# Attention: reciprocal spread and values in one bank, both issued behind a tile's second head, divisions sooner

## The chip, the cores and the metric

The kernel runs on one core of one Trainium2 chip. The metric is the device time of one execution in microseconds (us); the kernel before takes 1476.72 us (median of three runs, 1476.59 to 1477.12).

## The reference

One pre-norm decoder layer on x of shape (4, 512, 512): self-attention with 16 heads of width 32, then a cross-attention whose weights come from a context of width 256, then a feed-forward block with 4-bit weights. The part that matters here is the self-attention:

```
q, k, v = layernorm(x) @ Wq, @ Wk, @ Wv         # 16 heads of width 32
scores  = einsum('bthd,bshd->bhts', q, k) * tril   # masked entries are 0, not -inf
attn    = softmax(scores / sqrt(512), axis=-1)
x       = x + einsum('bhts,bshd->bthd', attn, v) @ Wo
```

Masked scores are zero and not minus infinity, so each row's denominator also holds a term for the tokens beyond the diagonal, and the values of those tokens are added with that one weight.

## The kernel before, in words

**The four batches.** The kernel walks over four batches (`body(n, last)` on each engine). In each, a stretch of about 62 us holds the softmax and the products with the values; around it lie the projections for the next batch and the mixing of this one (`between`). After the last batch comes the feed-forward block, a long dense run of TensorE matmuls.

**Units.** The softmax stretch is cut into 16 units. Unit u stands for four heads (group u // 4) and one tile of 128 query tokens (i = u % 4). A tile sees (i + 1) * 128 keys, so the widths of its four heads j = 0..3 are 128, 256, 384 or 512. The order of work on each engine is written out by hand as steps (u, j); nothing reorders it.

**One head of one unit** goes through these instructions. `scores` (TensorE, L932) writes bank j. `row_max` (VectorE, L1603) takes the maximum, GpSimd negates it (`shift`, L766), ScalarE takes the exponential (`exp`, L1260) into `prob`. `turn` (TensorE, L943) transposes it in blocks of 128 into one of three rotating banks, and `turned` copies that to `prob_t`: ScalarE for heads 0 to 2 (L1276; heads 0 and 1 only where i is 3), VectorE for the others (L1613). `scores(u + 1, j)` waits for `exp(u, j)`, because both use bank j.

**Once for each unit:** `reciprocals` (VectorE, L1631) makes `r_col`, one reciprocal for each token and head. `recips` (TensorE, L973) spreads them over the 32 rows of each head, eight matmul records. ScalarE copies the result to `r_den` (`recip_out`, L1282). `values` (TensorE, L964) multiplies `prob_t` with V into bank 6, in the half u % 2, with a last part for the tokens beyond the diagonal (`v_zero`, made by GpSimd, L776), and VectorE's `divide` (L1641) multiplies that half with `r_den` into `o_sum`. `values(u)` waits for `divide(u - 1)`. After a group's last unit ScalarE (`out_head`, L1288) and GpSimd (`out_tail`, L782) split `o_sum` in two half-precision parts.

**Repacking.** Beside this, TensorE transposes packed feed-forward weights in two halves (`repack`, L1039), at i = 0; ScalarE copies the first half (L1296), VectorE the second (L1654).

**The rotating banks.** `turn_bank(slot)` is one of banks 4, 5 and 7, by slot modulo 3. Each `turn`, each repacked half and, in the kernel before, each spread reciprocal (`recip_slot`) takes the next slot, and waits until the slot three before has been read (`turn_read`). In a unit without repacking the order of slots is T0 T1 T2 T3 R, where T is a head's transposes and R the reciprocals of the unit before.

**The order on TensorE in unit u:** before each turn(u, j) comes scores(u + 1, j). Behind turn(u, 1) stand both halves of the repacking where i = 0; behind turn(u, 3) come recips(u - 1) and values(u - 1). On ScalarE, step (u, j) is exp(u, j), then a copy of an earlier head. recip_out(v) stands in step (v + 2, 1), out_head in step 0 of a unit with i = 2. On VectorE divide(v) stands in step (v + 3, 0). At the end of a batch, TensorE also transposes the next batch's normalised input (`spread`, L892), with a copy by ScalarE (L1237) and a difference by VectorE (L1588).

Of the kernel before, what the change touches and what calls it, by code (L numbers as in the profile page):

```python
# [46 lines left out]
P = 128  # L47
# [44 lines left out]
def decoder_layer(nc, x, ctx_1024, Wq, Wk, Wv, Wo, xWq, xbq, xWk, xbk, gate_p, gate_s, up_p, up_s, down_p, down_s, out):  # L92
    with ExitStack() as ctx:
# [162 lines left out]
        den_done, rcol_done, r_full, rden_out = (sem(n) for n in ("den_done", "rcol_done", "r_full", "rden_out"))  # L256
# [22 lines left out]
        def turn_slot(h):  # L279


            return h + 2 * (max(0, h - 2) // 16) + max(0, h // 4 - 1)
# [13 lines left out]
        def pack_slot(r, half):  # L296
            return (turn_slot(16 * r + 17) + 1 if r < HG - 1 else recip_slot(UNITS - 2) + 1) + half

        def recip_slot(u):
            return turn_slot(4 * u + 7) + 1 if u < UNITS - 1 else pack_slot(HG - 1, 1) + 1  # L300
# [4 lines left out]
        def turn_read(n, slot):  # L305

            for u in range(UNITS):
                if slot == recip_slot(u):
                    return rden_out, n * UNITS + u + 1
# [12 lines left out]
        AT_RECIP, AT_DIVIDE = 9, 12  # L322
        AT_SUMS, AT_TURNED, AT_RECIPROCALS = 1, 3, 2
        AT_OUT = 0
# [347 lines left out]
        def _(pool):  # L672
# [155 lines left out]
            def body(n, last):  # L828
                for u in range(UNITS):
                    r, i = u // TT, u % TT  # L830
                    for j in range(4):
                        shift(n, u, j)
                        if j == 1 and u > 0 and i > 0:
                            masked_values(n, u - 1)
                        if j > 0 and i > 1:
                            convert(n * (NB // B) + r, r, 3 * i + j - 7)
                        if j == 3 and i == 2 and r > 0:
                            out_tail(n, r - 1)
# [37 lines left out]
        def _(pe):  # L876
# [69 lines left out]
            def values(n, u):  # L946
# [4 lines left out]
                if u == 0:  # L951
                    pe.wait_ge(v_out, n * TT + TT)
                if u >= 1:
                    pe.wait_ge(o_done, n * UNITS + u)
# [12 lines left out]
            def recips(n, u):  # L967

                slot = recip_slot(u)
                pe.wait_ge(*turn_read(n, slot - 3))  # L970
                pe.wait_ge(rcol_done, n * UNITS + u + 1)
                for j in range(4):
                    mm = pe.matmul(turn_bank(slot)[32 * j:32 * j + 32, 0:P], r_col[:, u % 2, j:j + 1].to_broadcast([P, DH]), ident[:], start=True, stop=True)  # L973
                mm.then_inc(r_full, 1)
# [53 lines left out]
            def repack(n, r):  # L1028
                nb = n * (NB // B) + r
                pe.wait_ge(pk_conv, 6 * nb + 6)  # L1030
                for half in range(2):
                    pe.wait_ge(*turn_read(n, pack_slot(r, half) - 3))
                    bk = turn_bank(pack_slot(r, half))[:].bitcast(F16)

                    tiles = [[(0, 0), (1, 0)], [(0, 1), (1, 1)], [(2, 0), (3, 0)]] if half == 0 else \
                            [[(2, 1), (3, 1)], [(4, 0), (4, 1)], [(5, 0), (5, 1)]]
                    for q in range(3):
                        for e, (a, w) in enumerate(tiles[q]):
                            mm = pe.transpose(bk[:, 256 * q + P * e:256 * q + P * e + P], pk_16[:, a, P * w:P * w + P], ident16[:])  # L1039
                    mm.then_inc(pk_full, 1)  # L1040
# [163 lines left out]
            def body(n, last):  # L1204
                for u in range(UNITS):
                    for j in range(4):
                        if u + 1 < UNITS:
                            scores(n, u + 1, j)
                        turn(n, u, j)
# [3 lines left out]
                        if j == 1 and u == UNITS - 1:  # L1213
                            values(n, u - 1)
                        if j == 3 and u > 0:
                            recips(n, u - 1)
                            if u < UNITS - 1:
                                values(n, u - 1)
                        if j == 1 and u % TT == 0 and u > 0:
                            repack(n, u // TT - 1)  # L1220
                repack(n, HG - 1)
# [11 lines left out]
        def _(act):  # L1233
# [44 lines left out]
            def recip_out(n, u):  # L1278
                act.wait_ge(r_full, n * UNITS + u + 1)
# [763 lines left out]
```

## Time and profile before

| | |
|---|---|
| median of three runs | 1476.72 us |
| profiled execution, its own time | 1477.48 us |
| its span in the trace | 1475.80 us |
| TensorE clock granted | 0.999 of full speed |
| softmax stretches in the span | about 71 to 133, 203 to 265, 335 to 397, 467 to 527 us |
| TensorE busy, whole span | 1424.5 us (97%) |
| ScalarE, VectorE busy, whole span | 716.9 us (49%), 990.3 us (67%) |

The profile is one execution on the chip. Its page gives busy times for the whole span; the stretch that the change touches is a sixth of it, and the views below are of that stretch. A matmul's record is longer than the time until the next matmul starts, so a busy share of TensorE is not its load. The same holds in a smaller measure for ScalarE and VectorE: each record reaches some tenth of a microsecond into the next one. So the text works with the time from one start to the next.

### The profile page before, as it was taken

The numbers are of one execution on the slowest core, as the hardware profiler recorded it, in microseconds if no ns is written. First come the engines' busy times: TensorE is split into PE (matmuls) and PEld (weight loads), VectorE is DVE, ScalarE is ACT, GpSimd is POOL, SyncE is SP. The second block draws the span as 40 slices with busy tenths as digits, with TensorE's granted clock in tenths as the row PEclk, the third lists the DMA queues.
The fourth block names the chain that finished last, engine by engine and source line by source line (L and its number), as shares of the span: only waits on it lengthen the run. The fifth ranks groups of instructions, "written<-read, shape, count | busy, mean of one in ns | idle before, by whom it ended". The sixth has DMA issues, their size and how long they took to land.

```text
span 1475.8 us, 26841 instructions
## 1 busy us (share of the span) xinstructions
PE 1424.5 (97%) x8896; PEld 719.7 (49%) x8896; DVE 990.3 (67%) x2125; ACT 716.9 (49%) x1660; POOL 380.3 (26%) x691
## 2 busy tenths in 40 slices
PE   6999998998999999999999999999999999999999
PEld 3465456556645654344444444444444444444444
DVE  7786688668658767886566666665655756665533
ACT  5795279339716945344354353353343443533532
POOL 0053225204374436521221212112112211212100
PEclk9999999999999999999999999999999999999999
DMA  7564522352465521000100001001001001000011
GB/s 249 134 168 125 162 79 81 101 162 79 126 176 156 180 80 46 17 28 22 32 14 21 17 17 33 17 17 35 17 17 32 17 16 33 17 17 1 0 58 57
DMA packets 77309, 98.01 MB, mean 66 GB/s; under 512 B 8048, under 2 KB 60784, under 8 KB 76784
## 3 DMA queue, kind: packets, MB, share of 16 engines
q1 hardware_dynamic: 77168, 96.23, 21.3%
q8 instruction: 76, 1.25, 0.4%
q14 instruction: 65, 0.53, 0.1%
HBM read 68.94 MB, written 27.26 MB: 65 GB/s over the span
## 4 chain that ended last, share of the span: by engine, by line
PE 85%; ACT 5%; issue 5%; DVE 4%; POOL 1%; DMA 0%; ACTq 0%; POOLq 0%; DVEq 0%; SPq 0%
PE bank L879 25%; PE bank L881 24%; PE bank L880 24%; ACT prob L1260 3%; PE bank L943 3%; PE bank L964 2%; PE bank L932 1%; PE bank L892 1%; PE bank L1004 1%; PE bank L1019 1%; PE bank L973 1%; PE bank L1014 1%; ACT prob_t L1276 1%; DVE xt L1588 1%; PE bank L1025 1%
## 5 line engine op out<-in xcount | busy, mean ns | idle before, releaser
L879 PE MATMUL bank<-xs,G 128*128 128x512 f16 x896 | 339.8, 379 | 2.1 <-DVE c L1733 1.0
L880 PE MATMUL bank<-xs,G 128*128 128x512 f16 x896 | 339.6, 379 | 0.0
L881 PE MATMUL bank<-xs,G 128*128 128x512 f16 x896 | 339.6, 379 | 0.0
L1348 ACT COPY c<-bank 128x512 f32<-128x512 f32 x192 | 111.4, 580 | 219.9 <-PE bank L881 215.1
L1733 DVE TENSOR_TENSOR c<-bank,c 128x512 f32<-128x512 f32 x128 | 88.1, 689 | 193.4 <-PE bank L881 193.4
L879 PE MATMUL bank<-Wd,hid 128*128 128x512 f16 x512 | 194.1, 379 | 2.8 <-DVE X L1787 2.8
L881 PE MATMUL bank<-Wd,hid 128*128 128x512 f16 x512 | 194.0, 379 | 0.0
L880 PE MATMUL bank<-Wd,hid 128*128 128x512 f16 x512 | 194.0, 379 | 0.0
L751 POOL TENSOR_TENSOR c<-c,m 128x512 f32<-128x512 f32 x64 | 82.3, 1287 | 388.9 <-ACT c L1348 388.9
L1787 DVE SCALAR_TENSOR_TENSOR X<-bank,col,X 128x512 f32<-128x512 f32 x128 | 95.4, 749 | 101.5 <-PE bank L881 101.4
L1603 DVE CUSTOM_DVE_ANT_0 bank<-bank,mask,col 128x128 f32<-128x128 f32 (+3 forms) x256 | 139.1, 548 | 23.4 <-issue 17.3
L1260 ACT ACTIVATE prob<-bank,nmx 128x128 f32<-128x128 f32 (+3 forms) x256 | 146.9, 582 | 0.7
L879 PEld LDWEIGHTS bank<-xs,G 128*128 128x128 f16 x896 | 87.7, 98 | 113.5 <-ACT c L1348 6.1
L881 PEld LDWEIGHTS bank<-xs,G 128*128 128x128 f16 x896 | 87.7, 98 | 105.7
L880 PEld LDWEIGHTS bank<-xs,G 128*128 128x128 f16 x896 | 87.7, 98 | 103.1
L943 PE MATMUL bank<-ident,prob 128*128 128x128 f32 x640 | 111.9, 277 | 12.9 <-ACT prob L1260 3.8
L1371 ACT CAST hid<-c 128x512 f16<-128x512 f32 x128 | 79.2, 619 | 90.3 <-DVE c L1747 87.2
L1363 ACT ACTIVATE c<-c,col 128x512 f32<-128x512 f32 x96 | 69.4, 723 | 94.1 <-DVE c L1733 94.1
L766 POOL TENSOR_TENSOR nmx<-zero,mx 128x1 f32<-128x1 f32 x256 | 51.1, 200 | 234.7 <-DVE mx L1603 208.6
L1753 DVE TENSOR_TENSOR hid<-c,hid 128x512 f16<-128x512 f32 x128 | 86.1, 712 | 25.7 <-ACT hid L1371 25.7
L708 POOL TENSOR_TENSOR w_sum<-w_full 128x384 f32<-128x384 f32 (+1 forms) x30 | 22.1, 738 | 314.0 <-DVE w_full L1714 313.8
L943 PEld LDWEIGHTS bank<-ident,prob 128*128 128x128 f32 x640 | 76.0, 140 | 30.8 <-issue 19.3
(192 smaller groups left out, 2408.3 us busy)
## 6 DMA issues: line engine op xcount, KB each, us to landing
stack<-qk_dram SPq DMA_DIRECT2D x128, 128.0 KB, 3.4
sc_in<-scale_t SPq DMA_DIRECT2D x30, 384.0 KB
qk_dram<-qk SPq DMA_DIRECT2D x32, 256.0 KB, 2.7
packed_t<-pk_t SPq DMA_DIRECT2D x32, 192.0 KB, 2.0
pk_in<-packed_t SPq DMA_DIRECT2D x30, 192.0 KB
X<-in_x_dram SPq DMA_DIRECT2D x4, 1024.0 KB, 5.9
pk_in<-L_ffn_gate_W_packed_dram SPq DMA_DIRECT2D x16, 256.0 KB, 2.7
pk_in<-n_L_ffn_up_W_packed_dram SPq DMA_DIRECT2D x16, 256.0 KB, 3.1
```

The source lines that it names most:

```text
L751: nc.gpsimd.tensor_tensor(c22[x][:], c22[x][:], m5[x][:], ALU.add).then_inc(c22_out, 1)
L879: pe.matmul(o, lhs(0), rhs(0), start=first, stop=False, skip_group_check=onto)
L880: pe.matmul(o, lhs(0), rhs(1), start=False, stop=False, skip_group_check=onto)
L881: return pe.matmul(o, lhs(1), rhs(0), start=False, stop=stop, skip_group_check=onto)
L943: mm = pe.transpose(turn_bank(slot)[:, P * k:P * k + P], prob[:, u % 2, j, P * k:P * k + P], ident[:])
L1260: nc.scalar.activation(prob[:, u % 2, j, 0:wide[i]], bank[j][:, 0:wide[i]], ACT.Exp, bias=nmx[:, u % 2, j:j + 1], accum_out=den[:, u % 2, ...
L1348: nc.scalar.copy(dst[:], bank[BANK_Y if which == M5 else x][:]).then_inc(c_copied, 1)
L1371: nc.scalar.copy(hid[:, beta, q, r, 0, :], quarter(1, idx)[:]).then_inc(hid_hi, 1)
L1603: nc.vector.tensor_tensor_reduce(out=bank[j][:, 0:wide[i]], in0=bank[j][:, 0:wide[i]], in1=mask[:, P * (3 - i):P * (3 - i) + wide[i]], sca ...
L1733: nc.vector.tensor_tensor(dst[:], bank[at][:], dst[:], ALU.add).then_inc(comb, 1)
L1753: nc.vector.tensor_tensor(hid[:, beta, q, r, 1, :], quarter(1, idx)[:], hid[:, beta, q, r, 0, :], ALU.subtract).then_inc(hid_lo, 1)
L1787: nc.vector.scalar_tensor_tensor(xv, bank[4 + t][:], C_OUT, xv, ALU.mult, ALU.add).then_inc(acc_out, 1)
```

## The change

The three rotating banks no longer carry the reciprocals. `recips(u)` writes the second half of bank 6 (columns 256 + 128 * (u % 2)), right ahead of `values(u)`, and only `values` signals. ScalarE's copy to `r_den` now waits for the values too, and VectorE's division waits for the copy. Both TensorE parts move from behind a unit's fourth head to behind its second (ahead of the second turn where i = 3). The copy of the reciprocals goes from step (v + 2, 1) to (v + 1, 3), the division from (v + 3, 0) to (v + 2, 2), or (v + 2, 3) for i = 0. The two halves of the repacking are parted, and `out_head`, `out_tail`, and VectorE's copy of the second half move with that.

```diff
         def turn_slot(h):
-            return h + 2 * (max(0, h - 2) // 16) + max(0, h // 4 - 1)
+            first_halves = sum(h > 16 * (r + 1) + 1 for r in range(HG - 1))
+            second_halves = sum(h > 16 * (r + 1) + 3 for r in range(HG - 1))
+            return h + first_halves + second_halves
         def pack_slot(r, half):
-            return (turn_slot(16 * r + 17) + 1 if r < HG - 1 else recip_slot(UNITS - 2) + 1) + half
-        def recip_slot(u):
-            return turn_slot(4 * u + 7) + 1 if u < UNITS - 1 else pack_slot(HG - 1, 1) + 1
+            return turn_slot(16 * (r + 1) + 1 + 2 * half) + 1 if r < HG - 1 else turn_slot(ROWS - 1) + 1 + half
-        AT_RECIP, AT_DIVIDE = 9, 12
+        AT_RECIP = 7
+        def divided_at(u):
+            return 4 * u + (11 if u % TT == 0 else 10)
...
@@ GpSimd, body
-                        if j == 1 and u > 0 and i > 0:
+                        if j == 1 and i == 2 and r > 0:
+                            out_tail(n, r - 1)
+                        if i > 0 and j == (2 if i == 2 else 1):
                             masked_values(n, u - 1)
...
-                        if j == 3 and i == 2 and r > 0:
-                            out_tail(n, r - 1)
...
@@ TensorE, values(n, u)
-                if u == 0:
-                    pe.wait_ge(v_out, n * TT + TT)
-                if u >= 1:
-                    pe.wait_ge(o_done, n * UNITS + u)
...
@@ TensorE, recips(n, u)
-                slot = recip_slot(u)
-                pe.wait_ge(*turn_read(n, slot - 3))
+                if u == 0:
+                    pe.wait_ge(v_out, n * TT + TT)
+                else:
+                    pe.wait_ge(o_done, n * UNITS + u)
                 pe.wait_ge(rcol_done, n * UNITS + u + 1)
+                at = P * (2 + u % 2)
                 for j in range(4):
-                    mm = pe.matmul(turn_bank(slot)[32 * j:32 * j + 32, 0:P], r_col[:, u % 2, j:j + 1].to_broadcast([P, DH]), ident[:], start=True, stop=True)
-                mm.then_inc(r_full, 1)
+                    pe.matmul(bank[6][32 * j:32 * j + 32, at:at + P], r_col[:, u % 2, j:j + 1].to_broadcast([P, DH]), ident[:], start=True, stop=True)
...
@@ TensorE, body
+                        ahead_of_turn = u % TT == TT - 1
+                        if j == 1 and u > 0 and ahead_of_turn:
+                            recips(n, u - 1)
+                            values(n, u - 1)
                         turn(n, u, j)
...
-                        if j == 1 and u == UNITS - 1:
+                        if j in (1, 3) and u % TT == 0 and u > 0:
+                            repack(n, u // TT - 1, j // 2)
+                        if j == 1 and u > 0 and not ahead_of_turn:
+                            recips(n, u - 1)
                             values(n, u - 1)
-                        if j == 3 and u > 0:
-                            recips(n, u - 1)
-                            if u < UNITS - 1:
-                                values(n, u - 1)
-                        if j == 1 and u % TT == 0 and u > 0:
-                            repack(n, u // TT - 1)
-                repack(n, HG - 1)
+                repack(n, HG - 1, 0)
+                repack(n, HG - 1, 1)
...
@@ ScalarE
             def recip_out(n, u):
-                act.wait_ge(r_full, n * UNITS + u + 1)
+                act.wait_ge(av_done, n * UNITS + u + 1)
...
-                        if j == AT_OUT and u % TT == 2 and u > TT:
-                            out_head(n, u // TT - 1)
...
+                        if j == 3 and u % TT == 1 and u > TT:
+                            out_head(n, u // TT - 1)
...
@@ VectorE
-                        h = 4 * u + j - AT_DIVIDE
-                        if h >= 0 and h % 4 == 0:
-                            divide(n, h // 4)
-                        if j == 0 and u % TT == 1 and u > TT:
+                        for v in range(UNITS):
+                            if divided_at(v) == 4 * u + j:
+                                divide(n, v)
+                        if j == 2 and u % TT == 1 and u > TT:
                             repacked(n, u // TT - 1)
...
-                divide(n, UNITS - 3)
```

## Rows read from the trace of the kernel before

**Rows 1.** The page: busy time of two engines, and the chain that ended last.
```profile
PE 1424.5 (97%) x8896; PEld 719.7 (49%) x8896; DVE 990.3 (67%) x2125; ACT 716.9 (49%) x1660; POOL 380.3 (26%) x691
...
PE 85%; ACT 5%; issue 5%; DVE 4%; POOL 1%; DMA 0%; ACTq 0%; POOLq 0%; DVEq 0%; SPq 0%
```

**Rows 2.** Busy time by stretch: start:end, length, engines, granted clock, DMA.
```profile
209.87:225.05 15.18, 13.81 (x206) 9.90 (x206) 12.52 (x50) 14.24 (x54) 7.52 (x26) 1.00 0.24 79
225.05:240.23 15.18, 13.66 (x206) 9.91 (x205) 12.83 (x53) 14.19 (x54) 7.49 (x26) 1.00 0.26 81
240.23:255.36 15.13, 13.60 (x205) 9.93 (x204) 12.43 (x51) 14.19 (x54) 7.09 (x26) 1.00 0.38 116
...
350.81:365.95 15.14, 13.62 (x213) 9.88 (x208) 12.85 (x54) 14.20 (x53) 7.50 (x27) 1.00 0.24 81
```

**Rows 3.** Groups by line and shape, 202 to 266 us: busy, mean ns, idle before.
```profile
L973 PE MATMUL bank<-ident,r_col 128*32 128x128 f32 x128 | 6.8, 284 | 0.0
...
L1282 ACT COPY r_den<-bank 128x128 f32<-128x128 f32 x16 | 4.7, 294 | 0.1
L1641 DVE SCALAR_TENSOR_TENSOR o_sum<-bank,r_den 128x128 f32<-128x128 f32 x16 | 4.6, 286 | 3.3 <-issue 2.4 <-PE bank L964 0.9
```

**Rows 4.** ScalarE in order of time: start, length, instruction, idle before it.
```profile
225.05 0.77 ACT L1260 ACTIVATE prob<-bank,nmx 128x512 f32<-128x512 f32 x1
...
226.14 0.73 ACT L1260 ACTIVATE prob<-bank,nmx 128x512 f32<-128x512 f32 x1
...
226.82 0.29 ACT L1282 COPY r_den<-bank 128x128 f32<-128x128 f32 x1
226.98 0.72 ACT L1260 ACTIVATE prob<-bank,nmx 128x512 f32<-128x512 f32 x1
...
231.32 0.27 ACT L1276 COPY prob_t<-bank 128x128 f32<-128x128 f32 x1 [0.54 <-PE bank L943]
...
232.08 0.82 ACT L1296 CAST pk_t<-bank 128x768 int16<-128x768 f16 x1
232.77 0.50 ACT L1260 ACTIVATE prob<-bank,nmx 128x256 f32<-128x256 f32 x1
...
235.15 0.37 ACT L1276 COPY prob_t<-bank 128x256 f32<-128x256 f32 x1 [0.43 <-PE bank L943]
```

**Rows 5.** TensorE in order of time, same columns.
```profile
227.88 0.63 PE L943 MATMUL bank<-ident,prob 128*128 128x128 f32 x4 [0.64 <-ACT prob L1260]
...
229.66 0.43 PE L973 MATMUL bank<-ident,r_col 128*32 128x128 f32 x8
229.91 0.84 PE L964 MATMUL bank<-prob_t,V 128*32 128x128 f32 x24
230.56 0.40 PE L964 MATMUL bank<-ident,v_zero 128*32 128x128 f32 x8
230.90 0.28 PE L932 MATMUL bank<-stack 128*128 128x256 f16 x1
```

**Rows 6.** VectorE in order of time, same columns.
```profile
224.80 0.29 DVE L1641 SCALAR_TENSOR_TENSOR o_sum<-bank,r_den 128x128 f32<-128x128 f32 x1 [0.81 <-issue]
...
227.18 0.55 DVE L1613 COPY prob_t<-bank 128x384 f32<-128x384 f32 x1
...
229.12 0.69 DVE L1613 COPY prob_t<-bank 128x512 f32<-128x512 f32 x1
...
232.21 0.56 DVE L1654 CAST pk_t<-bank 128x768 int16<-128x768 f16 x1 [0.16 <-PE bank L1039]
232.69 0.48 DVE L1603 CUSTOM_DVE_ANT_0 bank<-bank,mask,col 128x256 f32<-128x256 f32 x1
```

**Rows 7.** GpSimd in order of time, same columns.
```profile
223.55 1.16 POOL L782 TENSOR_TENSOR o_t<-o_sum,o_t 128x512 f16<-128x512 f32 x1
```

**Rows 8.** TensorE at the end of the second batch's softmax, same columns.
```profile
260.58 1.91 PE L892 MATMUL bank<-ident,xn 128*128 128x128 f32 x16
...
264.67 1.08 PE L964 MATMUL bank<-prob_t,V 128*32 128x128 f32 x32 [0.70 <-DVE o_sum L1641]
```

More of the change, by code:

```diff
@@ L255, in decoder_layer @@
         pt_act, pt_dve, av_done, o_done, o_hi, o_lo = (sem(n) for n in ("pt_act", "pt_dve", "av_done", "o_done", "o_hi", "o_lo"))
-        den_done, rcol_done, r_full, rden_out = (sem(n) for n in ("den_done", "rcol_done", "r_full", "rden_out"))
+        den_done, rcol_done, rden_out = (sem(n) for n in ("den_done", "rcol_done", "rden_out"))
         wo_full, x1_done, mix_full, x2_done = (sem(n) for n in ("wo_full", "x1_done", "mix_full", "x2_done"))
@@ L307, in turn_read @@
             for u in range(UNITS):
-                if slot == recip_slot(u):
-                    return rden_out, n * UNITS + u + 1
                 for j in range(4):
@@ L318, in decoder_layer @@
         CONTEXT_BANK = (6, 4, 5, 7)
-        AT_RECIP, AT_DIVIDE = 9, 12
+        AT_RECIP = 7
         AT_SUMS, AT_TURNED, AT_RECIPROCALS = 1, 3, 2
-        AT_OUT = 0
+        def divided_at(u):
+            return 4 * u + (11 if u % TT == 0 else 10)
         def beyond_units(n, u):
@@ L1026, in context_out, with repack @@
                     mm.then_inc(att_full, 1)
-            def repack(n, r):
+            def repack(n, r, half):
                 nb = n * (NB // B) + r
                 pe.wait_ge(pk_conv, 6 * nb + 6)
[L1031 to L1040, printed above, removed]
+                pe.wait_ge(*turn_read(n, pack_slot(r, half) - 3))
+                bk = turn_bank(pack_slot(r, half))[:].bitcast(F16)
+                tiles = [[(0, 0), (1, 0)], [(0, 1), (1, 1)], [(2, 0), (3, 0)]] if half == 0 else \
+                        [[(2, 1), (3, 1)], [(4, 0), (4, 1)], [(5, 0), (5, 1)]]
+                for q in range(3):
+                    for e, (a, w) in enumerate(tiles[q]):
+                        mm = pe.transpose(bk[:, 256 * q + P * e:256 * q + P * e + P], pk_16[:, a, P * w:P * w + P], ident16[:])
+                mm.then_inc(pk_full, 1)
             def product(m, x, which, pair, slot, nb):
@@ L1278, in recip_out @@
             def recip_out(n, u):
-                act.wait_ge(r_full, n * UNITS + u + 1)
+                act.wait_ge(av_done, n * UNITS + u + 1)
                 if u >= 2:
                     act.wait_ge(o_done, n * UNITS + u - 1)
-                nc.scalar.copy(r_den[:, u % 2, :], turn_bank(recip_slot(u))[:, 0:P]).then_inc(rden_out, 1)
+                nc.scalar.copy(r_den[:, u % 2, :], bank[6][:, P * (2 + u % 2):P * (3 + u % 2)]).then_inc(rden_out, 1)
             def out_head(n, hg):
@@ L1639, in divide @@
                 dve.wait_ge(rden_out, n * UNITS + u + 1)
-                dve.wait_ge(av_done, n * UNITS + u + 1)
                 nc.vector.scalar_tensor_tensor(o_sum[:, P * i:P * i + P], bank[6][:, P * (u % 2):P * (u % 2) + P], QS, r_den[:, u % 2, :],
```

## The prediction

> **What bounds the kernel now.** I read the page first: TensorE is busy 97% of the span and carries 85% of the chain that ended last [rows 1]. That is an average over a dense feed-forward and four softmax stretches, and the change touches only the latter. So I next read busy time by stretch. There the work repeats every four units. I call the time from the start of exp(u, 0) of one widest tile (u = 3, 7, 11, 15) to the next a cycle; there are three in a batch, twelve in all. A cycle takes 15.13 to 15.18 us, the clock is at its full 2.4 GHz level, and DMA moves little [rows 2]. The reader is to see that ScalarE has the highest busy share, 14.19 of 15.18 us, and TensorE 13.66.
>
> The timelines give the real load. On ScalarE a 512-wide exp is followed 0.68 us later and a copy of reciprocals 0.16 later [rows 4]; the exps of 128, 256 and 384 take 0.36, 0.46 and 0.56 from start to start, the copies 0.16, 0.26, 0.36 and 0.47 by width, e_zero 0.10, out_head 0.51, the repack copy 0.69. Over a cycle that is 8.24 + 0.30 + 3.26 + 0.64 + 0.51 + 0.69 = 13.64 us, so ScalarE waits 1.54 us in a cycle of 15.18. Neither engine is full; the cycle is set by waits between engines, and ScalarE's load is the floor. The two largest waits stand where TensorE comes late to the first transpose after a block of values: 0.54 us idle at 231.32 and 0.43 at 235.15, both about 0.65 from ScalarE's earliest possible start [rows 4].
>
> **The change part by part.** I take relative times, with zero at the start of exp(7, 0), 225.05 in the trace.
>
> *What it removes.* The rotating banks lose the reciprocals' slot. Before, turn(7, 1) had to wait until VectorE's copy of (6, 3) had read its bank: TensorE idles 0.64 us until 227.88 [rows 5], and 227.18 + 0.55 [rows 6] is 227.73, so it is this copy, although the profile names the exp that ended near by. Similar rotation waits precede turn(6, 0) and the third and fourth turns of unit 8. All are hidden or not according to ScalarE, so they are no sum by themselves. VectorE also loses 0.81 us of waiting at 224.80, where the division of a new group waits for GpSimd's out_tail of 1.16 us [rows 6, 7]; out_tail now starts two steps sooner. No work disappears: sixteen spreads, copies and divisions stay, at 0.25 us from the spread's start to the values' [rows 5], 0.16 and about 0.20 [rows 3].
>
> *What it adds.* I walked one cycle in the new order with the old durations. Delays from one engine to another are read off the same timelines: 0.04 us from a matmul's end to ScalarE, 0.12 from VectorE to TensorE, 0.31 from a row maximum to its exp, 0.10 of issue ahead of the spread and behind the values. Each item is a wait of ScalarE:
>
> 1. Turn(7, 1) now stands behind values(6), and these wait for the same copy of (6, 3), now done at 2.22. So values run 2.34 to 3.21 (32 matmuls, 0.87), turn(7, 1) starts at 3.31 against 2.83 before, and ScalarE, ready at 3.55, copies at 3.98: 0.43.
> 2. The later turn(7, 2) passes through VectorE's copy (0.60), reciprocals, the sooner division (0.20) and the maximum of (8, 3): exp(8, 3) can start at 6.08, ScalarE is ready at 5.85: 0.23.
> 3. The first repack half now follows VectorE's copy of (7, 3) in the rotation, done at 6.32. TensorE transposes from 6.44, ScalarE can copy at 6.97 and is ready at 6.69: 0.28.
> 4. recip_out(7) stands right behind that copy and now waits for the values, not for the spread alone. They run 7.11 to 7.98 behind the repack half, visible at 8.26; ScalarE is ready at 7.66: 0.60. Four exps of unit 9 and their copies queue behind it. exp(9, 0) starts at 8.42, before at 7.72 [rows 4].
> 5. scores(9, 2) is behind these values too. VectorE puts a division and the 0.48 us repack copy [rows 6] ahead of the maximum of (9, 3), so exp(9, 3) starts at 10.56, ScalarE ready at 10.22: 0.34. In return the 0.64 us wait of before at this place is gone.
> 6. turn(9, 1) waits for VectorE's copy of (8, 3) at 10.39, and recip_out(8) for the values behind it: 11.79 against 11.38: 0.41. out_head (0.51) is queued behind.
> 7. out_tail (1.16) [rows 7] is now between two negations of GpSimd and delays exp(10, 2): 0.18.
>
> The waits come to 2.47 us, with the load 13.64 + 2.47 = 16.11 us for a cycle, against 15.18: 0.93 us more. Twelve cycles: +11.2 us. In the first units of a batch item 6 in small costs 0.1 each: +0.4. At a batch's end the last values stood behind a division 0.70 us late [rows 8]; now the spread of 0.24 us also stands behind it, but the copy of (14, 3) comes 0.35 us sooner and turns 1 to 3 of unit 15 run unbroken, so the next batch's transposes can start at 4.7 after exp(15, 0), before at 260.58 - 255.36 = 5.2: -0.5 + 0.24 = -0.26 for each of four batches, -1.0. No DMA moves past another, and SP's queue keeps its order; repack stores start with the copies and have a whole cycle to land.
>
> Sum: 11.2 + 0.4 - 1.0 = +10.6 us. The profiled execution (span 1475.80, own time 1477.48) would become 1488.1; it stands 0.76 above the median, so the forecast is 1476.72 + 10.6 = 1487.3 us.
>
> *Bounds.* From below: if every ScalarE wait went, a cycle would be 13.64, 1.54 less, -18.5 us in twelve. From above: were each of items 1 to 7 late by another 0.08 us, a cycle would be 16.7, +18 us. I take the walk's value, since its delays are read from the nearest instructions of the same kind.
>
> A rule of the Trainium skill that speaks against the change is in its page "PSUM — Partial Sum Buffer", section "Terms": no two engines may use one bank and quadrant at once. Bank 6 now passes from TensorE to ScalarE to VectorE and back, where before the spread could be written while the division ran. By the rule the round is serial: spread and values 1.12, copy 0.27, division 0.28 [rows 3, 5] and four hand-overs of about 0.1, some 2.1 us, in a unit of 3.8. It fits; only where the division stands late in its queue does it bind. The trace of before agrees in so far as TensorE waits for a division [rows 8]. The sum above takes nothing from this page.
>
> **The rivals.**
>
> *A, faster.* TensorE's earlier values free the turns, and the waits of items 4 and 6 are covered because ScalarE arrives late, not early. For it: ScalarE is close to full (14.19 of 15.18 busy) [rows 2], and both big waits of before [rows 4] are for TensorE blocks that move away. Against it: items 4 and 6 are structural, since ScalarE needs 0.16 to 0.69 us from the second head's copy to the reciprocals' while TensorE needs 1.2 for spread and values. It decides if ScalarE reaches that copy over 0.5 us later than I think. Half of the waits gone: 12 x 0.77 + 1.0 = 10 us less, 1466.5 us.
>
> *B, no change.* Waits removed and added cancel: the cycle stays at 15.18, the time within 3 us of 1476.7. It needs 0.93 us of error in a walk of 16, all of one sign.
>
> *C, much slower.* The round of bank 6 binds. The place is recips(u) behind divide(u - 1): for the group's second division, it waits for out_tail, GpSimd's 1.16 us, behind ScalarE's out_head. If divide(8) ends later than 15.0 after the start (the walk says 14.2), TensorE holds turn and scores of unit 10. At 0.6 us more for each cycle: +7, in all +18, 1495 us.
>
> **How the numbers follow.** Forecast 0.48, C 0.12, B 0.12, A 0.28. A measurement of this kernel tells about 0.2%, 3 us, from no change. Faster is A: 0.28; same is B: 0.12; slower is the forecast and C: 0.60. The forecast's own range is 1480 to 1492. A spreads over 1458 to 1473, so a low end of 1465 leaves out 0.12 of it; C spreads to 1500, and 1496 leaves 0.06. Together that is the 8 in 10.
>
> **What would show it right or wrong.** The ScalarE timeline after the change should have a wait ahead of the reciprocals' copy in the first unit of a group (0.6) and in the second (0.4), put down to values, and cycles of 16.1 us in the windows. turn(7, 1) should start 0.5 us later after exp(7, 0) than now. If cycles are near 14.5 and ScalarE has no idle time but at a group's start, A holds. If TensorE idles ahead of the spread for the division, C holds. A changed clock, or a changed feed-forward time after the fourth batch, would be outside all of them.

## The result, and the profile after

The changed kernel takes 1493.17 us (median of four runs, 1492.49 to 1493.63) against 1476.69 us for the kernel before (four runs, 1476.59 to 1477.12): ratio 1.0110, 95% interval 1.0097 to 1.0123. It is 16.5 us slower. The forecast was slower by 10.6 us, 1487.3 us. The time lies in the range given (1465 to 1496), but 1.2 us above the forecast's own range.

The page of the kernel after, its lines that answer to [rows 1]:

```profile
PE 1423.0 (95%) x8896; PEld 720.7 (48%) x8896; DVE 990.5 (66%) x2125; ACT 719.5 (48%) x1660; POOL 381.8 (26%) x691
...
PE 83%; DVE 6%; ACT 5%; issue 5%; DMA 0%; DVEq 0%; ACTq 0%; POOL 0%; SPq 0%
```

No engine executes more instructions than before, and the busy times differ by at most 0.4%; the span is longer (1490.9 us), so it is waiting that was added. The cycles of batch 2, as [rows 2]:

```profile
213.76:230.49 16.73, 14.43 (x209) 10.39 (x208) 13.12 (x52) 14.44 (x54) 7.96 (x28) 1.00 0.23 73
230.49:246.97 16.48, 13.79 (x205) 10.02 (x204) 13.09 (x52) 14.44 (x53) 7.62 (x27) 1.00 0.23 74
246.97:263.45 16.48, 13.78 (x205) 10.01 (x204) 12.24 (x50) 14.45 (x53) 7.19 (x27) 1.00 0.36 106
```

A cycle takes 16.48 us where the walk said 16.11, and the first of each batch 16.73 (16.94 in the first batch). The granted clock is 1.00 in all three, its 2.4 GHz level, as before.

ScalarE after, the middle cycle, its starts after a wait (start, length, instruction, idle before it; the cycle begins at 230.49). Line numbers moved: 1259 is `exp`, 1275 `turned`, 1281 `recip_out`, 1295 the repack copy.

```profile
230.49 0.72 ACT L1259 ACTIVATE prob<-bank,nmx 128x512 f32<-128x512 f32 x1
...
234.49 0.59 ACT L1275 COPY prob_t<-bank 128x512 f32<-128x512 f32 x1 [0.31 <-PE bank L943]
...
236.57 0.37 ACT L1259 ACTIVATE prob<-bank,nmx 128x128 f32<-128x128 f32 x1
...
237.49 0.80 ACT L1295 CAST pk_t<-bank 128x768 int16<-128x768 f16 x1 [0.21 <-PE bank L1036]
238.75 0.27 ACT L1281 COPY r_den<-bank 128x128 f32<-128x128 f32 x1 [0.46 <-PE bank L960]
...
241.06 0.47 ACT L1259 ACTIVATE prob<-bank,nmx 128x256 f32<-128x256 f32 x1 [0.24 <-POOL nmx L766]
...
242.32 0.27 ACT L1281 COPY r_den<-bank 128x128 f32<-128x128 f32 x1 [0.34 <-PE bank L960]
...
244.87 0.58 ACT L1259 ACTIVATE prob<-bank,nmx 128x384 f32<-128x384 f32 x1 [0.35 <-POOL nmx L766]
```

There is one row for each of the seven items of the prediction. The idle time in brackets is short of the true wait by the tenth or two that a record reaches into the next one, so the table takes the wait as the prediction did: this start, less the previous start and its price from start to start.

| item | what starts late | start after exp(7, 0): forecast | measured | wait: forecast | measured |
|---|---|---|---|---|---|
| 1 | copy of turn(7, 1) | 3.98 | 4.00 | 0.43 | 0.49 |
| 2 | exp(8, 3) | 6.08 | 6.08 | 0.23 | 0.24 |
| 3 | repack copy | 6.97 | 7.00 | 0.28 | 0.31 |
| 4 | recip_out(7) | 8.26 | 8.26 | 0.60 | 0.57 |
| 5 | exp(9, 3) | 10.56 | 10.57 | 0.34 | 0.38 |
| 6 | recip_out(8) | 11.79 | 11.83 | 0.41 | 0.44 |
| 7 | exp(10, 2) | 14.02 | 14.38 | 0.18 | 0.49 |

Up to 12 us into the cycle the walk is right within 0.05 us. Then item 7 is 0.31 too small. What items 1, 3 and 6 wait for stands in TensorE's order of time, same columns:

```profile
233.80 0.66 PE L943 MATMUL bank<-ident,prob 128*128 128x128 f32 x4
...
236.96 0.49 PE L1036 MATMUL bank<-ident,pk 128*128 128x128 f16 x6 [0.55 <-DVE prob_t L1611]
...
241.05 0.41 PE L943 MATMUL bank<-ident,prob 128*128 128x128 f32 x2 [0.56 <-DVE prob_t L1611]
```

The first row is turn(7, 1), at 3.31, as forecast, against 2.83 before [rows 5]. The other two are the repack half and turn(9, 1), both waiting for VectorE's copy of the slot three before, at 6.47 (forecast 6.44) and 10.56 (forecast for the copy 10.39).

What the walk missed is on GpSimd, same columns:

```profile
243.18 1.16 POOL L782 TENSOR_TENSOR o_t<-o_sum,o_t 128x512 f16<-128x512 f32 x1 [0.63 <-ACT o_t L1287]
244.29 0.40 POOL L759 CAST pk<-pk_in 128x256 f16<-128x256 uint8 x1
244.64 0.19 POOL L766 TENSOR_TENSOR nmx<-zero,mx 128x1 f32<-128x1 f32 x1
```

Between out_tail and the negation for exp(10, 2) stands a conversion of packed weights (`convert`, 0.35 from start to start). The diff shows it in the lines around the moved call; the walk had out_tail followed by the negation at once.

### The profile page after: what moved, and what is told of

Same layout as the page of the kernel before. It is cut to its first block, busy times and chain, and to the rows that moved or that the text cites. A ratio compares the mean times of both kernels' runs of the same rounds, so it can differ in the third digit from the quotient of the medians.

```text
span 1490.9 us, 26745 instructions
## 1 busy us (share of the span) xinstructions
PE 1423.0 (95%) x8896; PEld 720.7 (48%) x8896; DVE 990.5 (66%) x2125; ACT 719.5 (48%) x1660; POOL 381.8 (26%) x691
## 4 chain that ended last, share of the span: by engine, by line
PE 83%; DVE 6%; ACT 5%; issue 5%; DMA 0%; DVEq 0%; ACTq 0%; POOL 0%; SPq 0%
PE bank L879 24%; PE bank L881 24%; PE bank L880 24%; ACT prob L1259 3%; PE bank L943 2%; PE bank L960 2%; PE bank L932 1%; PE bank L972 1%; PE bank L892 1%; PE bank L1017 1%; PE bank L1002 1%; ACT prob_t L1275 1%; PE bank L1012 1%; DVE bank L1601 1%; DVE xt L1586 1%
## 5 line engine op out<-in xcount | busy, mean ns | idle before, releaser
L1259 ACT ACTIVATE prob<-bank,nmx 128x128 f32<-128x128 f32 (+3 forms) x256 | 138.0, 550 | 9.3 <-POOL nmx L766 7.9
L932 PE MATMUL bank<-stack 128*128 128x128 f16 (+3 forms) x256 | 75.5, 305 | 20.7 <-ACT prob L1259 18.2
```

The source lines that it names most:

```text
L932: pe.matmul(bank[j][:, 0:wide[i]], stack[:, 0, h, P * i:P * i + P], stack[:, 1, h, 0:wide[i]], start=True, stop=True).then_inc(s_full, 1)
L1259: nc.scalar.activation(prob[:, u % 2, j, 0:wide[i]], bank[j][:, 0:wide[i]], ACT.Exp, bias=nmx[:, u % 2, j:j + 1], accum_out=den[:, u % 2, ...
```

## The experiments

Each kernel was timed beside the kernel before on the same chip: 1477.12 us for the first four, 1476.98 for the next four, 1476.59 for the last two (1476.69 for the changed kernel). "Cycle" is the second one of batch 2. "Batches" is the time from the first exp of batch 1 to the first matmul behind the last values of batch 4, in us more than in the kernel before (459.80). Both are from the one profiled execution of each kernel. The differences between two kernels in the text below are between their medians where nothing else is said, taken on different chips in part; the medians of the kernel before show how much that can be, 0.5 us.

| kernel | us (lowest to highest) | ratio, 95% | cycle, us | batches |
|---|---|---|---|---|
| changed kernel | 1493.17 (1492.49-1493.63) | 1.0110 (1.0097-1.0123) | 16.48 | +16.5 |
| convert first | 1491.09 (1490.24-1491.97) | 1.0095 (1.0078-1.0112) | 16.27 | +14.5 |
| positions alone | 1493.21 (1492.16-1494.20) | 1.0109 (1.0092-1.0126) | 16.06 | +13.9 |
| bank alone | 1479.77 (1479.34-1480.69) | 1.0021 (1.0011-1.0031) | 15.52 | +3.6 |
| values late | 1466.03 (1465.20-1466.46) | 0.9926 (0.9909-0.9942) | 14.32 | -10.8 |
| copy later | 1493.21 (1492.96-1493.93) | 1.0111 (1.0094-1.0128) | 16.36 | +16.2 |
| pack copy later | 1487.91 (1487.20-1489.22) | 1.0076 (1.0060-1.0093) | 16.02 | +11.0 |
| early values, late copies | 1511.74 (1510.58-1512.86) | 1.0238 (1.0221-1.0255) | 17.66 | +34.6 |
| late order, own bank | 1482.80 (1481.98-1484.10) | 1.0042 (1.0026-1.0059) | 15.57 | +3.7 |
| both mended | 1485.62 (1485.40-1486.80) | 1.0061 (1.0048-1.0075) | 15.82 | +9.0 |
| late values only | 1468.57 (1468.27-1469.65) | 0.9945 (0.9931-0.9959) | 14.59 | -7.6 |

**Convert first.** GpSimd's conversion ahead of out_tail, all else as in the changed kernel.

```diff
-                        if j == 1 and i == 2 and r > 0:
-                            out_tail(n, r - 1)
+                        if j == 1 and i == 2:
+                            convert(n * (NB // B) + r, r, 3 * i + j - 7)
+                            if r > 0:
+                                out_tail(n, r - 1)
...
-                        if j > 0 and i > 1:
+                        if j > 0 and i > 1 and (i, j) != (2, 1):
```

> The changed kernel, with GpSimd's conversion of the packed weights in step (4r + 2, 1) put ahead of out_tail instead of behind it. In the changed kernel exp(6, 2) waits 0.35 us for its negation, which stands behind out_tail (1.16 us) and this conversion (0.40 us, from start to start 0.35). Theory 1 (item 7 of the prediction was 0.18 and is mis-sized because the conversion was left out): the wait falls from 0.35 to 0.0 to 0.1, a cycle from 16.48 to about 16.2, the whole by 2 to 4 us, to 1489 to 1491. Rival (another wait follows at once, and the cycle is set elsewhere): the wait goes, cycle and time stay, 1493.

Measured 1491.09, 2.1 us less than the changed kernel (2.0 by the batches of the traces). In GpSimd's order of time:

```profile
242.70 0.39 POOL L759 CAST pk<-pk_in 128x256 f16<-128x256 uint8 x1
243.38 1.16 POOL L782 TENSOR_TENSOR o_t<-o_sum,o_t 128x512 f16<-128x512 f32 x1 [0.29 <-ACT o_t L1289]
244.50 0.19 POOL L766 TENSOR_TENSOR nmx<-zero,mx 128x1 f32<-128x1 f32 x1
```

exp(10, 2) starts at 244.72, 14.16 into a cycle that begins at 230.56, and waits 0.13: item 7 falls from 0.49 to 0.13, so the conversion was 0.36 of it. The cycle is shorter by 0.21 only, because the copy of turn(7, 1) is now at 4.13 instead of 4.00: 0.13 comes back as a larger item 1 at the start of the next cycle. VectorE's rows show one step of the way:

```profile
230.72 0.76 DVE L1603 CUSTOM_DVE_ANT_0 bank<-bank,mask,col 128x512 f32<-128x512 f32 x1 [0.30 <-PE bank L934]
```

This maximum waits 0.30 for its scores and starts 0.16 after the cycle's start, where in the changed kernel it started 0.07 ahead of it. All that follows it on VectorE is 0.23 later by the cycle's clock, the copy of (6, 3) for which item 1 waits among it (1.77 instead of 1.54). Why TensorE's scores are not sooner as well I did not trace.

**Positions alone.** The new places of everything, but the spread in a rotating slot of its own, as before the change; the slots were numbered by the new order.

```diff
-                at = P * (2 + u % 2)
+                slot = recip_slot(u)
+                if slot >= 3:
+                    pe.wait_ge(*turn_read(n, slot - 3))
...
-                    pe.matmul(bank[6][32 * j:32 * j + 32, at:at + P], ...)
+                    mm = pe.matmul(turn_bank(slot)[32 * j:32 * j + 32, 0:P], ...)
+                mm.then_inc(r_full, 1)
```

> Half of the change alone: all engines in the new order, but the spread reciprocals keep their own slot in the rotating banks, and ScalarE's copy waits for the spread and not for the values. Theory 1 (the new positions cause most of the loss, through TensorE blocks that stand ahead of the turns and scores that ScalarE needs; the copy's wait for the values adds a part): cycles of 16.0 to 16.2, 1488 to 1491, so over two thirds of the 16.5 us loss stays. Rival (the loss is the copy's wait for the values in bank 6, items 4 and 6, 1.0 us of 2.5): cycles of 15.2 to 15.4 and 1477 to 1481.

**Bank alone.** The kernel before with only the bank changed: spread in bank 6, right ahead of the values behind the fourth head (unit 14's behind the second), every step elsewhere as before.

```diff
-            return h + 2 * (max(0, h - 2) // 16) + max(0, h // 4 - 1)
+            return h + 2 * (max(0, h - 2) // 16)
...
-                act.wait_ge(r_full, n * UNITS + u + 1)
+                act.wait_ge(av_done, n * UNITS + u + 1)
```

> The other half alone: the kernel before, with the spread in the second half of bank 6 directly ahead of the values and ScalarE's copy waiting for the values, every position as before (but the spread of unit 14 goes with its values, behind the second head of unit 15). Theory 1: ScalarE's copy in step (v + 2, 1) now waits for values that end about 1 us later than the spread at a group's start; the freed slot gives back some 0.3: a cycle 0.3 to 0.5 longer, 1480 to 1483. Rival (the freed slot is worth more than the wait, as the change may have meant): 1472 to 1475. Rival (bank and position do harm only together): 1476.7.

Positions alone took 1493.21, as long as the whole change and above the range expected, and bank alone 1479.77, 2.7 more than before and just below its range. So the places carry most of the loss: 13.9 of 16.5 us by the batches. But it is not the same loss: with its own slot the middle cycle is 16.06, 0.42 below the changed kernel's (the copy of the reciprocals waits for the spread alone, so items 4 and 6 are small), and the four batches together are 2.6 us shorter by the trace. The part of the trace behind the fourth batch is 4.3 us longer (952.4 against 948.1), 2.6 of it a single pause of TensorE, 491 us behind the fourth batch. Why it is there is open; it means that the equal medians of these two kernels are a coincidence. In the kernel with the bank alone the waits say what the shared signal costs (view of the waits, 204 to 272 us: waiter and releaser, us in total, times, longest):

```profile
ACT r_den L1272 <- PE bank L955: 6.2, 7, 1.8
```

In ScalarE's order of time, in the cycle that begins at 226.54:

```profile
232.53 0.27 ACT L1272 COPY r_den<-bank 128x128 f32<-128x128 f32 x1 [0.89 <-PE bank L955]
...
236.37 0.27 ACT L1272 COPY r_den<-bank 128x128 f32<-128x128 f32 x1 [0.56 <-PE bank L955]
```

Before, ScalarE's copies of reciprocals had no such wait to speak of [rows 3]; here they wait for the values. In the changed kernel it is 2.4 in total. In the same cycle TensorE stands idle too, 0.43 ahead of scores(8, 3), for an exp, with values(6) still to come.

**Values late.** From the kernel with the bank alone. "Late" is meant against the change. The spread and the values go ahead of the fourth turn where i = 0, behind the third turn where i = 3, and behind the fourth head where i = 1 or 2. So they are later than in the changed kernel, but in two of the four units of a cycle sooner than in the kernel before and in bank alone, where all of them stand behind the fourth head. The idea was to put each block where TensorE would have to wait in any case. The two halves of the repacking are parted as well.

```diff
+                        behind = 1 if u == UNITS - 1 else 2 if u % TT == TT - 1 else 3
+                        ahead_of_turn = u % TT == 0
+                        if j == 3 and u > 0 and ahead_of_turn:
+                            recips(n, u - 1)
+                            values(n, u - 1)
                         turn(n, u, j)
...
-                        if u > 0 and j == (1 if u == UNITS - 1 else 3):
+                        if j in (0, 3) and u % TT == 0 and u > 0:
+                            repack(n, u // TT - 1, j // 3)
+                        if u > 0 and j == behind and not ahead_of_turn:
                             recips(n, u - 1)
                             values(n, u - 1)
-                        if j == 1 and u % TT == 0 and u > 0:
-                            repack(n, u // TT - 1)
```

VectorE's copy of the repacked half goes to step 3 of the unit with i = 1; the copies of reciprocals and the divisions keep the steps of the kernel before.

> Bank 6 as in the change, but spread and values late: ahead of the fourth turn where i is 0, behind the fourth where i is 1 or 2, behind the third where i is 3; the repack halves behind the first and the fourth head of i = 0, VectorE's copy of the second half in step (4r + 1, 3); copies of reciprocals and divisions in the steps of before. Theory 1 (what costs is TensorE work put ahead of turns and scores that ScalarE waits for; what helps is the freed slot, if values fill the time in which TensorE waits for an exp): cycles of 14.0 to 14.6 and 1463 to 1470, faster than before. Rival (a spread in bank 6 always loses, since ScalarE waits for the values): over 1477.

It took 1466.03 us: 11.1 less than the kernel before beside it, 27 less than the changed one. Busy time by stretch, middle cycle:

```profile
221.79:236.11 14.32, 13.30 (x205) 9.89 (x205) 12.94 (x52) 14.11 (x53) 7.49 (x26) 1.00 0.25 86
```

ScalarE's record time of 14.11 is all but the cycle, against the load of 13.64 from start to start; 0.68 us of waits are left of 1.54. TensorE's idle times in this cycle are short. The longest:

```profile
234.24 0.39 PE L927 MATMUL bank<-stack 128*128 128x512 f16 x1 [0.29 <-ACT prob L1255]
```

**Copy later.** ScalarE's copy of the reciprocals one step later, where the values have been done for long; it takes away items 4 and 6 by themselves.

```diff
-        AT_RECIP = 7
+        AT_RECIP = 8
```

> The changed kernel with ScalarE's copy of the reciprocals one step later, in step (v + 2, 0) and not (v + 1, 3). Items 4 and 6 of the prediction, the waits of this copy for the values (0.46 and 0.34 us idle in the changed kernel's trace, 0.6 and 0.4 from the earliest start), should shrink, since an exp and a transposed head's copy now run ahead of it. Theory 1 (the items add up): a cycle falls by 0.8 to 1.0 to about 15.6, the whole to about 1482. Rival (the round of bank 6: a later copy makes the division and so the next spread later, and ScalarE then waits for turns instead): cycles of 16.2 to 16.5, 1491 to 1494, no gain.

It took 1493.21, no gain. The rows show where the wait went. On ScalarE, in order of time (the cycle begins at 230.11):

```profile
231.15 0.31 ACT L1281 COPY r_den<-bank 128x128 f32<-128x128 f32 x1
...
234.73 0.59 ACT L1275 COPY prob_t<-bank 128x512 f32<-128x512 f32 x1 [0.76 <-PE bank L943]
```

And on VectorE:

```profile
231.49 0.29 DVE L1638 SCALAR_TENSOR_TENSOR o_sum<-bank,r_den 128x128 f32<-128x128 f32 x1 [0.38 <-ACT r_den L1281]
```

Items 4 and 6 are gone. But the division of unit 5 now waits for the later copy and starts at 1.38 after the cycle's start instead of 0.70. Everything in VectorE's queue behind it is late, the copy of (6, 3) among it, on which values(6) and then turn(7, 1) wait: the copy of turn(7, 1) is at 4.62 instead of 4.00. Item 1 grows from 0.49 to 0.95 and takes back most of what item 4 gave (0.57). A wait that the changed kernel did not have takes back most of item 6 (0.44): the copy of turn(9, 0) comes 0.40 late. The cycle is 0.12 shorter, and the batch's end 0.7 longer (10.53 from exp(15, 0) to the next projections, against 9.81).

**Pack copy later.** VectorE's copy of the second repacked half one step later, behind the maximum of (9, 3) in the cycle shown, so that item 5 loses its 0.47 us.

```diff
-                        if j == 2 and u % TT == 1 and u > TT:
+                        if j == 3 and u % TT == 1 and u > TT:
                             repacked(n, u // TT - 1)
```

> The changed kernel with VectorE's copy of the second repack half in step (4r + 1, 3), behind the maximum of (4r + 1, 3), and not ahead of it. Item 5 of the prediction: exp(4r + 1, 3) waits for its maximum behind this copy (0.48). Theory 1: this maximum starts 0.48 sooner, exp(9, 3) is no longer late, and turn(9, 1) follows VectorE's copy of (8, 3) as before or sooner: a cycle 0.3 to 0.5 shorter, about 16.0 to 16.2, 1487 to 1489. Rival (the copy only moves behind: the division or turn(9, 2), which takes its slot, waits instead): 1492 to 1494.

It took 1487.91, 5.3 us less than the changed kernel (5.5 by the batches). exp(9, 3) starts at 10.19 instead of 10.57, recip_out(8) at 11.38 instead of 11.83, and all to the cycle's end is 0.46 sooner: 16.02. Item 5 was there, in its size, and 0.07 of item 6 hung on it. Nothing took it back.

**Early values, late copies.** The kernel with late values, but TensorE's spread and values behind the second head as in the change; the repacking stays as in values late, and everything on the other engines too, with copies of the reciprocals and divisions at the steps of the kernel before.

```diff
-                        behind = 1 if u == UNITS - 1 else 2 if u % TT == TT - 1 else 3
-                        ahead_of_turn = u % TT == 0
-                        if j == 3 and u > 0 and ahead_of_turn:
+                        behind = 1
+                        ahead_of_turn = u % TT == TT - 1
+                        if j == 1 and u > 0 and ahead_of_turn:
```

> The fast kernel of the fourth run with only the places of spread and values on TensorE taken from the change (behind the second head, ahead of the second turn where i is 3); copies of reciprocals and divisions stay in the steps of before. It tells whether early values or the copies' early place do the harm. Theory 1 (the copies' wait for the values): the copy comes long after the values, so no such wait, cycles of 14.5 to 15.2 and 1467 to 1477. Rival (the round of bank 6: the spread must wait for the division of the unit before, which now is late for it, and turns and scores queue behind the waiting spread): cycles over 16.5, above 1495, slower than the whole change.

It took 1511.74. From the view of the waits, 204 to 272 us:

```profile
PE bank L967 <- DVE o_sum L1635: 10.8, 13, 1.7
ACT prob_t L1271 <- PE bank L938: 9.0, 13, 1.2
```

The longest in one cycle, in TensorE's order of time (L967 is `recips`):

```profile
234.57 0.42 PE L967 MATMUL bank<-ident,r_col 128*32 128x128 f32 x8 [1.59 <-DVE o_sum L1635]
```

This is rival C's mechanism, alive: the spread waits for the division in nearly every unit. So the early values need the sooner copies and divisions. Whether those would gain anything of their own, with the values left late, no run shows.

**Late order, own bank.** The order of the late values, but the spread in a rotating slot of its own (edit as for positions alone).

> The fast kernel of the fourth run with the spread back in its own slot of the rotating banks and ScalarE's copy waiting for the spread alone. With before, the third run and the fourth it makes a table of bank by order. Theory 1 (order and freed slot help only together, since with the slot a turn behind the repack half waits for VectorE's or ScalarE's copies again): cycles of 14.8 to 15.2, 1474 to 1478, as before. Rival (the late order alone does it): 1464 to 1469.

It took 1482.80, which neither had: the late order is 5.8 us slower than before when the spread still takes a slot. Of these, 3.7 are in the batches. Behind the fourth batch this trace is longer too (950.5 against 948.6 before), with a pause of TensorE of 2.9 us at the same place as with positions alone. TensorE waits at the spread (L982), at turns (L952) and once at a repacked half (L1047) for the reader of the slot three before. From the waits, 204 to 272 us:

```profile
ACT prob_t L1287 <- PE bank L952: 4.3, 9, 0.8
...
PE bank L982 <- ACT pk_t L1307: 2.2, 3, 0.7
...
PE bank L952 <- DVE prob_t L1624: 1.3, 4, 0.6
PE bank L1047 <- ACT r_den L1293: 1.1, 1, 1.1
```

**Both mended.** The changed kernel with convert first and pack copy later together.

> The changed kernel with both repairs at once: GpSimd's conversion ahead of out_tail (alone: 1491.1 us, 2.1 less) and VectorE's copy of the repacked half one step later (alone: 1487.9, 5.3 less). If the forecast's items add up, both gains come: the cycle goes from 16.48 to about 15.83 us and the time to 1493.2 - 2.1 - 5.3 = 1485.8 us (1485 to 1487). Rival: the two waits stand in one chain (exp(9, 3) late, then everything of unit 10 late), so that the second gain is mostly swallowed by the first: 1487.5 us or more, cycle 16.0.

It took 1485.62, as the sum of the two says (1485.8); by the batches 2.0 and 5.5 alone, 7.5 together. exp(9, 3) is at 10.20, exp(10, 2) at 13.72 instead of 14.38, the cycle 15.82. The 0.13 that convert first had lost in item 1 is not lost here.

**Late values only.** Values late, with the repacking back as before: both halves behind the second head, VectorE's copy at its old step.

```diff
-                        if j in (0, 3) and u % TT == 0 and u > 0:
-                            repack(n, u // TT - 1, j // 3)
+                        if j == 1 and u % TT == 0 and u > 0:
+                            repack(n, u // TT - 1, 0)
+                            repack(n, u // TT - 1, 1)
```

> The kernel that took 1466.0 us, with the repacking back where the kernel before has it: both halves behind the second head of i = 0, VectorE's copy at its old step. What is left of that kernel is bank 6 for the spread and the late places of the values. Theory: the places of the values carry the gain over the kernel with bank 6 alone (1479.8 us), because each block of values then lies right ahead of a turn that would wait for its bank anyway; the repacking's two places give a small part: cycle 14.6 to 14.9 us, 1469 to 1474 us. Rival: the gain is the parting of the two repacked halves, which no longer take two rotating slots in a row; then this one stays near 1479 us, cycle 15.4.

It took 1468.57, just below the range of the first theory (1469 to 1474). Each against the kernel before beside it, bank alone is at +2.7, this one at -8.0 and values late at -11.1 us. So of these 13.7 us, 10.7 are the two places of the values (ahead of the fourth turn where i = 0, behind the third where i = 3), and 3.1 the parted repacking.

The rows say what the two places give. In bank alone the values of unit 6 start 4.88 us after the cycle's start and those of unit 7 at 8.71; here 3.73 and 7.59. The waits of 0.89 and 0.56 ahead of ScalarE's copies of these reciprocals are gone, TensorE's idle time of 0.43 ahead of scores(8, 3) is filled by values(6), and the cycle goes from 15.52 to 14.59. So against the kernel before it is values moved up by a little that gain.

The two edits of the change crossed, with the order of values late beside them, in us against the kernel before on the same chip. In brackets is the same by the batches alone, since the part behind them was longer in two of these traces:

| | order of before | order of the change | late order |
|---|---|---|---|
| spread in a rotating slot | 0 | +16.1 (13.9) | +5.8 (3.7) |
| spread in bank 6 | +2.7 (3.6) | +16.5 (16.5) | -11.1 (-10.8) |

## Why the prediction was right in direction and short in size

**What bounds the kernel.** Held. The cycle is set by waits between engines above ScalarE's load: 16.48 less the seven measured waits (2.92) leaves 13.56, against 13.64 read before. Values late shows that 14.32 can be had.

**Items 1 to 6.** Held one by one, within 0.06 us, together 2.43 us against 2.29. Item 5 is shown by pack copy later, items 4 and 6 by their rows and by copy later, in which they are gone. The reading that [rows 5]'s wait before turn(7, 1) is for VectorE's copy and not for the exp that the profile named is borne out by the cycle in which the copy is late: in the first one of the batch it starts 0.34 later than in the second, and values(2) start 0.22 later (2.54 against 2.32 after the cycle's start), with 0.48 between the spread's start and theirs instead of 0.24.

**Item 7 is the term that failed in size.** "Out_tail (1.16) is now between two negations of GpSimd and delays exp(10, 2): 0.18" left out the conversion that stands behind out_tail in the same step. It measured 0.49; with the conversion ahead of it 0.13. The size is off by 0.31 a cycle, 3.7 us of the 5.9 that the cycles lack.

**The sum.** By the trace the twelve cycles cost 199.0 us against 181.8, +17.1, forecast +11.2. Beside item 7 there are 1.2 us in the first cycles of the batches: 0.25 each, and 0.46 in the first batch. In the first cycle of batch 2 all of its 0.24 is in item 1: the copy of turn(3, 1) comes at 4.24, because VectorE comes out of the batch's start late (its copy of (2, 3) starts 1.88 after the cycle's start, against 1.54 in the next). The walk took one cycle and multiplied it by twelve. The rest is 0.14 a cycle more from items 1 to 6, 0.08 a cycle less from a load read too high (13.64, measured 13.56), and 0.3 us from taking 15.18 for all cycles of before. Two small slips of the reading moved nothing: the copies of transposed heads add up to 3.28 by their prices, not 3.26, and the wait at 235.15 is 0.55 from ScalarE's earliest start, not 0.65.

**The batch's start** was put at +0.1 each and is +0.28 (6.34 against 6.06 from exp(1, 0) to exp(3, 0)): two copies of reciprocals lie in this stretch instead of one (0.17), and the two start some 0.1 late in all. I had looked for waits there and not counted the moved copy.

**The batch's end** was put at -0.26 each, -1.0. It is -0.29, -0.52, -0.28 and -0.66, together -1.75 us. The spread for the next batch starts 4.58 after exp(15, 0) (forecast 4.7). In TensorE's order of time, as [rows 8]:

```profile
268.03 1.91 PE L892 MATMUL bank<-ident,xn 128*128 128x128 f32 x16
...
272.03 0.42 PE L972 MATMUL bank<-ident,r_col 128*32 128x128 f32 x8 [1.42 <-DVE o_sum L1638]
```

The wait for the division, 0.70 before, is 1.42, and now holds back the spread of the reciprocals too. Yet the next projections start sooner, 9.81 after exp(15, 0) against 10.33. VectorE's rows show why the longer wait costs nothing: the division for which it waits (271.70) stands behind four differences for the next batch (from 269.30), and these follow TensorE's transposes, which begin 0.64 sooner than before.

In all +17.1 + 1.1 - 1.75 = +16.5, as much as the difference of the medians. The two profiled executions differ by 15.2 in their spans, since the opening of the kernel up to exp(1, 0) of the first batch is 0.84 shorter and the rest behind the fourth 0.47 shorter in that of after; the opening lies anywhere between 70.7 and 71.9 us in the traces of these kernels, so that the two numbers agree this closely is in part chance.

**Rival A** fell for this change. It needed ScalarE to reach the second head's copy 0.5 us later than in the walk; it reached recip_out(7) at 7.69, the walk had 7.66. Its reason was right, that the blocks of values cost waits where they stand in [rows 4] and that sooner values would free the turns. Values late and late values only collect it: they move the block up too, in two of four units, but by less than the change does, and leave ScalarE 0.68 us of waits in a cycle instead of 1.54 (values late). That values late takes 1466.0 and rival A had 1466.5 is chance; its number was for the order of the change.

**Rival B** needed cancellation; nothing cancelled. **Rival C** gave the nearest number, 1495, but not by its mechanism: the division of unit 8 ends at 14.2, as in the walk, and in the cycles TensorE never waits for a division. With early values and late copies and divisions it does, and costs 46 us over values late.

**The rule on banks.** That two engines may not use one bank and quadrant at once is what the Trainium skill states ("PSUM — Partial Sum Buffer", section "Terms"). No run here breaks the rule, so none shows what would happen; the kernels keep it by their own waits. What the serial round costs came out as weighed: it fits where the order leaves room (bank alone +2.7 us, values late -11), and binds where the division is late (early values, late copies: TensorE waits 10.8 us for divisions in that view).

**Do items add up?** Where a wait is removed by an edit that delays nothing else, yes: pack copy later and convert first give 5.3 and 2.1 alone, 7.6 together. Where the same edit makes an instruction late for somebody else, no: copy later removes two items of together 1.0 us a cycle and gains 0.12.

## What to carry to other kernels

Walk the order of every engine through the changed stretch, with each instruction that the loops issue in it, also those that the change doesn't touch: most of what item 7 lacked was one conversion left out of GpSimd's 27 instructions of a cycle, while the other six items were right within 0.06 us. A freed buffer slot and an order can be worth something only together: here the slot alone costs 2.7 us, the order of values late alone 5.8 (3.7 in the batches), both save 11. A block of work in an in-order queue has a best place between what it holds up and what waits for it. The change, which puts it behind the second head, cost 16.5 us, part of it in turns and scores that stood behind it; a step ahead of its old place in two of four units it filled time in which TensorE stood idle, and gained 10.7. Look for such a gap in the timeline and move the block there, and no further.

## What the runs showed that was not expected

- A rotation wait has no fixed name in the profile. TensorE's wait for the copy of (6, 3) stood under ScalarE's exp before; after the change waits of the same kind are named VectorE's `prob_t`.
- One gain came back smaller by a path that isn't in the walk: convert first made item 1 larger by 0.13 in every cycle, and with pack copy later added it did not.
- The part behind the fourth batch is 948.1 to 948.6 us in the traces of ten of the kernels (before and after among them), but 952.4 with positions alone and 950.6 with late order, own bank. The work there is the same. Each of the two has one pause of TensorE there, 2.65 and 2.88 us, ending 491 us behind the fourth batch, ahead of a matmul for whose start the profile names no other engine. The kernel before has one of 0.93 us at the same place, the other nine none. The two share the edit that keeps the spread in its own slot under a new numbering. The cause is open: one trace of each is kept, and no experiment was made on it.
